# Conditioned mixing, a signed layer and a low-rank layer on one core: scale products apart from the logits and mixing product

## What is computed

```python
# block 0
h = gelu(gelu(cond @ W0 + b0) @ W1 + b1)
att = softmax(h @ W2 + b2)                       # 32 x 8
agg_w, agg_b = einsum(att, weight), att @ bias_k # a 64 x 64 mixing matrix and a bias for each batch
y = einsum("boi,bih->boh", agg_w, x) + agg_b
routing = softmax(y @ gate_w.T)                  # 8 experts for each token
x = x + ((y * (routing @ in_scale)) @ sign(weight).T) * (routing @ out_scale) + bias
# block 1
z = conv1d(x, 9 taps, 4 groups) + context(cond)
x = x + z @ W.T + b + sum over experts of softmax(q.k) * (z @ A) @ B     # q = z @ Wq, k = z @ Wk
```

## Time and profile before

| what | value |
|---|---|
| median of the runs | 557.45 us (3 runs: 559.61, 555.99, 557.45) |
| the profiled execution | 560.03 us |
| its span in the profile | 558.0 us |
| granted clock, mean | 0.991 |
| busy: TensorE products / weight loads | 538.6 us (97%) / 461.9 us (83%) |
| busy: VectorE / ScalarE / GpSimd | 254.7 / 123.4 / 155.5 us |
| moved | 66.79 MB, mean 120 GB/s |

### The profile page before, as it was taken

How to read it: one execution, slowest core, us unless ns; L and a number is a source line. 1 busy time by engine, 2 the same in 40 slices (tenths; PEclk the granted TensorE clock), 3 DMA queues, 4 the chain that set the end, 5 groups by cost and what they waited for, 6 DMA issues and landing times.

```text
span 558.0 us, 13990 instructions
## 1 busy us (share of the span) xinstructions
PE 538.6 (97%) x5717; PEld 461.9 (83%) x5717; DVE 254.7 (46%) x461; ACT 123.4 (22%) x289; POOL 155.5 (28%) x79
## 2 busy tenths in 40 slices
PE   5879999999999899999999999999999999999997
PEld 4657788787887798898988988989889899898896
DVE  4439888797775762323224332242232322422321
ACT  5614434343434320101101011011011110110100
POOL 0027776767758490110101101011011010110100
PEclk9989999999999989999999999999999999999999
DMA  8684565555558451330412303204033032130100
GB/s 311 241 330 159 172 204 187 197 197 187 204 172 215 132 185 43 81 104 17 119 51 66 117 14 103 95 22 118 38 80 113 4 118 78 40 118 39 39 39 38
DMA packets 38775, 66.79 MB, mean 120 GB/s; under 512 B 4384, under 2 KB 25056, under 8 KB 38752
## 3 DMA queue, kind: packets, MB, share of 16 engines
q1 hardware_dynamic: 38528, 66.09, 36.3%
q10 hardware_dynamic: 224, 0.36, 0.3%
HBM read 49.64 MB, written 16.79 MB: 119 GB/s over the span
## 4 chain that ended last, share of the span: by engine, by line
PE 92%; DVE 3%; DMA 2%; ACT 1%; issue 1%; SPq 0%; DVEq 0%; ACTq 0%
PE bank L587 52%; PE bank L491 19%; PE bank L566 8%; PE bank L622 4%; PE bank L425 3%; DMA xs<-in_x 2%; PE bank L438 2%; PE bank L467 2%; DVE parts L912 1%; DMA cst<-in_consts 1%; ACT late L693 1%; PE bank L448 0%; PE bank L455 0%; PE bank L473 0%; ACT parts L724 0%
## 5 line engine op out<-in xcount | busy, mean ns | idle before, releaser
L587 PE MATMUL bank<-early,parts 128*128 128x320 f32 (+1 forms) x1152 | 208.2, 339 | 1.8 <-DVE parts L912 1.8
L587 PEld LDWEIGHTS bank<-early,parts 128*128 128x128 f32 x1152 | 186.1, 189 | 18.7 <-issue 2.2
L491 PE MATMUL bank<-late,parts 128*128 128x512 f32 x512 | 131.1, 408 | 1.5 <-ACT parts L724 1.5
L1101 POOL TENSOR_TENSOR work<-work,bias_bc 128x1024 f32<-128x1024 f32 x16 | 38.0, 2375 | 279.2 <-DMA work<-x_scratch 279.2
L491 PEld LDWEIGHTS bank<-late,parts 128*128 128x128 f32 x512 | 95.0, 193 | 22.6 <-ACT parts L724 1.7
L587 PE MATMUL bank<-late,parts 128*128 128x512 f32 x384 | 94.1, 394 | 0.0
L587 PEld LDWEIGHTS bank<-late,parts 128*128 128x128 f32 x384 | 70.9, 188 | 15.9
L912 DVE TENSOR_TENSOR parts<-y_t,parts 128x512 fp32r<-128x512 f32 x64 | 59.4, 931 | 12.3 <-ACT parts L724 11.0
L724 ACT ACTIVATE parts<-y_t 128x512 fp32r<-128x512 f32 x64 | 39.7, 633 | 98.7 <-DVE y_t L995 67.0
L1066 POOL TENSOR_TENSOR work<-work 128x512 f32<-128x512 f32 x32 | 45.9, 1436 | 49.4 <-DVE work L920 48.2
L1016 DVE TENSOR_TENSOR qk<-bank,qk 128x256 f32<-128x256 f32 x16 | 6.8, 425 | 104.6 <-ACT qk L810 104.6
(11 more groups left out here) (91 smaller groups left out, 351.0 us busy)
## 6 DMA issues: line engine op xcount, KB each, us to landing
xs<-in_x SPq DMA_DIRECT2D x16, 512.0 KB, 3.4
work<-in_x SPq DMA_DIRECT2D x16, 512.0 KB, 3.3
x_scratch<-work SPq DMA_DIRECT2D x16, 512.0 KB, 3.0
raw<-x_scratch SPq DMA_DIRECT2D x128, 64.0 KB, 3.0
work<-x_scratch SPq DMA_DIRECT2D x16, 512.0 KB, 3.7
out_tokens<-work SPq DMA_DIRECT2D x15, 512.0 KB, 2.7
stage<-in_wearly SPq DMA_DIRECT2D x8, 576.0 KB, 3.9
row_bc<-token_rows_scratch SPq DMA_DIRECT2D x30, 64.0 KB, 3.2
```

The source lines that it names most:

```text
L491: last = mm(bank[4 + h][:, :], parts[:, p, a, c, :], signs[:, c, h * HALF:(h + 1) * HALF], start=(k % 16 == 0), stop=(k % 16 == 15))
L587: return mm(dst, parts[:, p, a, c, :], w(b, c), start=(k == 0), stop=(close and k == 23))
L1101: g.tensor_tensor(resid[:, p, :], resid[:, p, :], bias_bc[:, :], ALU.add).then_inc(resid_ready, 1)
```

## The change

The block in front of step 18 becomes two: the logits of `two` and the mixing product of `three` stand in front of step 10, the scale products of `one` stay in front of step 18. The order of the three among each other is the same, and so are all waits. The other engines' programs are unchanged. It holds for all periods except that of the tile (0, 0).

```diff
-TURN_AT, BLOCK_AT, SUM_AT, CONV0_AT = 7, 18, 26, 8
+TURN_AT, BLOCK_AT, SCALES_AT, SUM_AT, CONV0_AT = 7, 10, 18, 26, 8
...
                             product_logits(*two)
                         if three:
                             product_y(*three)
+                    if k == SCALES_AT:
                         product_scales(*one, copied=2 if two else 1)
                     if k == SUM_AT and two:
                         sum_logits(*two)
```

## The result

The changed kernel takes 559.59 us (median of 19 executions, 557.17 to 563.58), the kernel before 557.16 us (19, 554.16 to 559.61). The ratio is 1.0054, with a 95% interval of 1.0036 to 1.0071: 2.0 to 4.0 us slower, about half a percent. This cannot be read from the two profiled executions alone, which took 560.0 us after and 560.03 before.

The account below looks back on a forecast made before the run. TensorE was taken as the bound, 92% of the chain. New borders in 11 periods at 0.20 us add 2.2 us, other terms 0, to the median 557.45, giving 559.6 us; range 556.9 to 562.3.

Parts of the forecast that it names:

- (a): All engines: same instructions and DMAs in the same number; only TensorE's order differs, logits and mixing product 8 steps earlier.
- (b): TensorE's signed steps: splitting the run of 11 into 3 and 8 adds borders costing 0.20 us a period, bounds 0 and 0.40.
- (c): Ahead of step 10: no wait for biased y or mixing matrix, 0 us; margin 0.6, tightest 0.15 in the second period.
- B: Rival, chance 0.07: bias sums come later than step 10 in six periods, costing 2.4 to 5.1 us more, 562 to 564.7.
- (d): VectorE's output scaling comes about 1.7 us later, filling its 1.90 us idle gap with 0.3 us left; cost 0.
- (e): Tile 13's period: the 0.44 us wait for the logits copy goes, but lengthens the wait before the second stage; gain 0.
- (f): Second period's turning: its 0.39 us routing wait, set by VectorE behind GpSimd, absorbs the first period's 0.20 us once.
- Rival A: TensorE's new exit and entry cost no more than pitches, so borders are hidden: 557.4 us, at best 557.0; chance 0.15.
- D: Rival, chance 0.08: the run of 3 steps lacks queued weights, each new border costs 0.39 us on both sides; 561.0.
- C: Rival, chance 0.10: the half-rate clock stretch behind the wait before the second stage, costing 1.7 us, doubles: 561.3; if it vanishes, 557.9.

Follow-up runs that it names:

- later loads: Second convolution input's eight loads issued behind tile 15's residual storing and reloading in SP's queue: on the kernel before 554.29 us (0.9953), on the changed kernel 556.97 us (0.9989).
- three blocks: Changed kernel split once more: logits at step 10, mixing product at 14, scale products at 18; 561.79 us, ratio 1.0104 to the kernel before.
- two lone products: Kernel before plus one overwritten product ahead of step 13 in twelve periods: 128x128 weights like the steps' 559.97 us (1.0050), 64x64 weights 562.91 us (1.0103).
- turning beside the logits: Changed kernel with the routing's turning at step 10, right ahead of the logits, instead of step 7; 559.31 us, ratio 1.0053 to the kernel before.
- one block at 14: Kernel before with its one block (logits, mixing product, scale products) moved unsplit from step 18 to 14; 561.2 us, ratio 1.0078.
- both small edits: Kernel before with the second convolution input's loads issued later and tile 13's logits at step 10; 554.48 us, ratio 0.9962.

## Why the prediction was right

I forecast 559.6 us for a kernel that takes 559.59; such closeness is luck. The forecast was 2.2 us on top of 557.45; measured are 2.4 between the medians, on top of 557.16, and the ratio's interval spans 2 us. By its steps:

(a), (b) Right, and mis-sized by a little. The new exit and entry were set at 0.20 us a period, the periods show 0.23. Of that 0.21 is where I put it (0.89 + 2.04 against 2.72); the rest is in the run behind the scale products, which I took as unchanged (130.16 to 132.11 is 1.95, before 1.93). The changed kernel, with and without the later loads, and the one with three blocks agree on 0.23 for a split. The two lone products show what is paid: ahead of a block the whole 0.09 belongs to the change of form, but of the 0.11 behind it only 0.03 does; the other 0.08 a product of the steps' own form costs too. So a little over half of a split's cost is the form's. The sentence that the three products cost the same apart as together holds to 0.01 us. I had weighed a rule of the Trainium skill: "TensorEngine Tiling (Array Packing)", section Key Properties, says that a change of tiling mode drains TensorE. The run with the turning beside the logits agrees with it, and so do the two lone products, whose weights were loaded 0.22 us ahead with the same form and not ahead at all with the other. The page gives no figure for the cost.

(c) Right for the bias. There is no wait for it in the steady periods. In the second period, where the margin was put at 0.15 us, the bias sums ended at 51.84 + 1.29 = 53.13 and the logits began at 53.34, a margin of 0.21; B did not come about. The sentence on the mixing matrix, that it was made one period earlier, fails in the first period: there TensorE waited 0.42 us for it, as told above. A wait of 0.47 us for the same matrix stands there in the run with the turning beside the logits, and none in the other two kernels that have logits at step 10 in this period.

(d) Right to a tenth of a microsecond. VectorE's output scaling now waits for TensorE and the scaling of y follows with 0.35 us to spare, where 0.3 was forecast:

```profile
129.22 0.69 DVE L921 TENSOR_TENSOR work<-bank,work 128x512 f32<-128x512 f32 x1 [1.67 <-PE bank L491]
130.26 1.29 DVE L906 TENSOR_TENSOR y_t<-bank,y_t 128x512 f32<-128x512 f32 x2 [0.35 <-PE bank L467]
```

The output scaling runs 129.22 - 124.97 = 4.25 us behind the turning instead of 2.50, the 1.7 us that were worked out.

(e) Right in what came of it: the gain of 0.3 us at tile 13 exists and was lost in the wait ahead of the second stage. The chain I gave, from the bias sums by x1's storing and loading to GpSimd, lacked its longest link: the sixteen loads of the convolution inputs, which held the SP queue for 8.82 us ahead of the store. The experiment with the later loads shows it, as the wait goes with the order of that queue alone. The wait itself became 2.77 us and not the 2.1 to 2.3 forecast. In this execution the residual's load, issued at 185.23, let GpSimd start at 190.45, 5.2 us later; before it was 189.42 - 185.62 = 3.8. One more link differs: before, VectorE's L912 stood behind GpSimd's difference and ended last; in the changed kernel the difference came later, VectorE was done by 190.2, and TensorE waited for GpSimd's L1071 itself.

(f) Open. The first period's waits depend on when the start lets TensorE begin: with the block at step 18, undivided, it took 10.20 us in the run that reached it latest (46.55) and 11.64 in one that reached it at 42.96; divided it took 10.79 to 11.76. With this scatter no run separates 0.2 us in it. Nor was it tested that GpSimd, and not TensorE, sets the wait at the second turning.

Rival A (hidden borders) falls by the periods, D (0.33 us a period) also. C, the clock: behind the wait 3.4 us ran at half rate before and after alike (0.66 over 196 to 201), so it made no difference here. I had priced that stretch at 1.7 us; the 48 products took 8.81 and 8.80 us with it and 7.27 or 7.28 in the runs that waited without it, so it cost 1.5. Whether the clock falls varies between executions (below). The sum over the periods, 2.52 us, lies in the interval of the whole, 2.0 to 4.0.

## What to carry to other kernels

When TensorE's stream is dense, small products of another weight form should stand together: each further place at which they interrupt the main products cost 0.23 us here, in each of twelve periods. A product of the main form costs less at its borders, nothing ahead of it and 0.08 us behind. Before moving a block, look for what its place covers (here a ScalarE copy), since the uncut move can cost as much as cutting it. And when a gain of TensorE vanishes, look at the next wait behind it: here it belonged to eight loads in the SP queue that nobody needed yet, and putting them later gained 1.1 to 4.1 us, while no order of the products tried here gained anything that shows in the time.

## What was not expected of the hardware

The start varies by microseconds between executions of the same instructions, with the clock: between 36 and 42 us the granted clock was 0.52 before, 1.00 after, 0.81 in the run with one block at 14 and 0.50 in the run with both small edits, and from the turning in the very first tile's steps to that of the first period it took 11.25 to 17.74 us over all runs. Medians of many executions carry the comparison; two profiles don't.

Behind the wait ahead of the second stage the clock fell in four of the eight profiled executions that waited (waits of 1.84, 1.85, 2.35 and 2.77 us; the 48 products then took 8.80 or 8.81 us) and not in the other four (waits of 2.02 in three and 2.44 us; 7.27 or 7.28 us). In the three without a wait it didn't fall (7.20 us).

One VectorE subtraction of 128x512 (L912), 0.69 us as a rule, took 3.14 us in the earlier trace rows while GpSimd's 3.10 us difference ran from 0.5 us before it, and 1.70 us while GpSimd's L1066 ran (at 53.24 us, before). Both ended 0.55 us behind the GpSimd instruction. No run takes GpSimd's work away, so that one holds up the other is argued and not shown. I had not priced it; if it is so, it is part of why the end of the stage hangs on GpSimd.
